# A graph attention layer on one core: GpSimd multiplies chunks 2 and 3 of x for the second table, in place of VectorE

## The reference

```python
in_fts = W @ x.T
f1 = (w1 @ in_fts).T + b1          # one number for each row
f2 = (w2 @ in_fts).T + b2          # one number for each column
bias_mat = where(adj > 0, 0.0, -1e9)
coefs = softmax(leaky_relu(f1 + f2.T) + bias_mat, axis=-1)   # slope 0.01
out = layernorm(x + coefs @ x, axis=-1)
```

## Time and profile before

| | |
|---|---|
| median of 3 runs | 275.73 us (275.19 to 277.98) |
| the profiled execution | 275.53 us, its span 273.8 us |
| busy share: PE, PEld, DVE, ACT, POOL | 94%, 82%, 89%, 72%, 23% |
| granted TensorE clock | full (mean 0.999) |
| HBM read, written | 71.37 MB, 2.10 MB |

### The profile page before, as it was taken

One profiled execution on the slowest core, in us unless ns is written; L12 is line 12 of the kernel. 1 busy time (PEld: TensorE's weight loads), 2 busy tenths in 40 slices (PEclk: granted clock), 3 DMA queues, 4 the chain that ended last, 5 costly groups with the idle time before them and its releaser, 6 DMA issues.

```text
span 273.8 us, 5925 instructions
## 1 busy us (share of the span) xinstructions
PE 257.2 (94%) x2163; PEld 223.8 (82%) x2163; DVE 244.6 (89%) x316; ACT 195.9 (72%) x285; POOL 64.0 (23%) x92
## 2 busy tenths in 40 slices
PE   2999969799999999999999999999999999999991
PEld 2989747688888888888888888888888888888880
DVE  1898999996998899999999999999999999999943
ACT  2669999939999999997499729982998196012140
POOL 2000045940000015201620063006300630063330
PEclk9999999999999999999999999999999999999999
DMA  6999999999999999999999999999999999501020
GB/s 188 275 294 314 321 323 284 263 260 314 329 326 327 328 327 326 346 345 328 316 331 342 327 302 230 339 315 314 293 347 326 320 238 341 143 0 38 1 60 19
DMA packets 22502, 73.64 MB, mean 269 GB/s; under 512 B 3030, under 2 KB 4184, under 8 KB 22488
## 3 DMA queue, kind: packets, MB, share of 16 engines
q1 hardware_dynamic: 11184, 35.17, 42.6%
q10 hardware_dynamic: 9960, 34.64, 41.4%
q0 software_dynamic: 1344, 3.67, 4.9%
HBM read 71.37 MB, written 2.10 MB: 268 GB/s over the span
## 4 chain that ended last, share of the span: by engine, by line
DVE 63%; DMA 12%; issue 10%; POOL 5%; ACT 5%; ACTq 1%; DVEq 1%; PE 0%; POOLq 0%
DVE mn L718 20%; DVE msk L731 11%; DVE mn L723 11%; DMA nat<-in_adj 11%; ACT sgn L462 4%; DVE post L839 3%; DVE ybt L854 2%; DVE bns L859 2%; DVE ntot L844 2%; DVE post L841 2%; DVE bt L708 2%; DVE post L702 2%; DMA msk<-in_x 1%; POOL ea L372 1%; DVE msk L736 1%
## 5 line engine op out<-in xcount | busy, mean ns | idle before, releaser
L1075 PE MATMUL ps<-bt,msk 128*128 128x258 f16 x2048 | 232.1, 274 | 4.5 <-DVE msk L731 2.8
L1075 PEld LDWEIGHTS ps<-bt,msk 128*128 128x128 fp8e5 x2048 | 200.6, 98 | 35.3 <-issue 4.1
L462 ACT ACTIVATE sgn<-f2b,nf1l 128x1024 int8<-128x1024 f32 x128 | 136.5, 1147 | 6.2 <-POOL flag L395 4.8
L718 DVE TENSOR_SCALAR mn<-nat 128x4096 int8<-128x4096 int32 x32 | 73.1, 2283 | 3.0 <-DMA nat<-in_adj 2.5
L402 POOL TENSOR_SCALAR nmr<-mv 128x4 f32<-128x4 f32 x7 | 12.8, 1834 | 141.1 <-DVE mv L863 141.1
L731 DVE STREAM_TRANSPOSE msk<-mn 128x1024 uint32<-128x1024 uint32 x32 | 39.8, 1245 | 2.6
L723 DVE SCALAR_TENSOR_TENSOR mn<-sgn,mn 128x1024 uint32<-128x1024 uint32 x32 | 39.2, 1225 | 3.3 <-ACT sgn L462 2.3
L591 ACT ACTIVATE ybt<-ybt,nmr,rstd 128x128 f32<-128x128 f32 x28 | 11.5, 483 | 33.2 <-POOL nmr L407 33.2
L584 ACT ACTIVATE post<-ps,ac 128x258 f32<-128x258 f32 x60 | 25.0, 471 | 14.1 <-PE ps L1075 14.1
L736 DVE TENSOR_SCALAR msk<-msk 128x1024 uint32<-128x1024 uint32 x32 | 22.2, 695 | 1.0
L413 POOL DMA_DIRECT2D out<-ybt x24 | 13.7, 570 | 16.3 <-ACT ybt L591 14.9
(11 more groups left out here) (109 smaller groups left out, 105.7 us busy)
## 6 DMA issues: line engine op xcount, KB each, us to landing
nat<-in_adj SPq DMA_DIRECT2D x64, 512.0 KB, 13.8
nat<-in_adj ACTq DMA_DIRECT2D x64, 512.0 KB, 16.3
xn<-in_x POOLq DMA_DIRECT2D x4, 512.0 KB, 19.8
out<-ybt POOLq DMA_DIRECT2D x24, 64.0 KB, 6.7
msk<-in_x SPq DMA_DIRECT2D x8, 128.0 KB, 3.8
msk<-in_x ACTq DMA_DIRECT2D x8, 128.0 KB, 4.5
out<-ybt SPq DMA_DIRECT2D x4, 64.0 KB, 1.8
out<-post SPq DMA_DIRECT2D x4, 32.0 KB, 1.6
```

What stands on the lines that cost most here:

```text
L462: ins = act.activation(sgn[:, c, g * JA:(g + 1) * JA], f2b[:, :], ACT.Sign, bias=nf1l[:, bass.ds(G * t + g, 1)], scale=-1.0)
L718: dve.tensor_scalar(mn[:, c % 2], nat[:, c], 0, EDGE, ALU.is_gt, ALU.mult).then_inc(cast_done, 1)
L1075: ins = pe.matmul(ps[:, 2 * c + m, 0:2 * DV], mask_f[c][m][:, n // KB, n % KB, :], btv[m][:, n, :], start=(n == 0), stop=(n == NK - 1))
```

## The change

The multiplies of chunks 2 and 3 for table m=0 leave VectorE's list and go to GpSimd's, as `tensor_tensor` with the same operands (128 x 1024 f32, both inputs in SBUF), ahead of its four loads of `xn` and of the flag's 17 instructions. Each waits for table_ready[1] to reach h+1, so for `low_x(1, 2)` and `low_x(1, 3)`. `split_x(0, 2)` and `split_x(0, 3)` wait for the new semaphore y_pool. `plus(0, 0)` moves one place forward on VectorE, to where `scale_x(0, 2)` stood. ScalarE's, TensorE's and SP's lists have the same instructions in the same order.

```diff
@@ GpSimd's list @@
+            pool.wait_ge(cs_ready[0], 1)
+            for h in range(2, BCH):
+                pool.wait_ge(table_ready[1], h + 1)
+                part = slice(h * CN, (h + 1) * CN)
+                pool.tensor_tensor(ybuf[:, h], xl_chunk(h), cs[:, 0, part, None].to_broadcast([P, CN, D]),
+                                   ALU.mult).then_inc(y_pool, 1)
+
             pool.wait_ge(f1_made, 2)
             pool.wait_ge(cast_done, 2)
             for g in range(G):
@@ split_x on ScalarE @@
                 elif m == 0:
-                    act.wait_ge(y_ready[0], h - 1)
+                    act.wait_ge(y_pool, h - 1)
@@ VectorE's list @@
             dve.wait_ge(cs_ready[0], 1)
             low_den(0)
-            scale_x(0, 2)
+            plus(0, 0)
             stat_max(1, 2, 4)
-            scale_x(0, 3)
-            plus(0, 0)
             low_x(0, 0)
@@
-            dve.wait_ge(y_ready[0], 2)
+            dve.wait_ge(y_pool, 2)
             turn(3, 3)
```

More of the change, by code:

```diff
@@ L200, in gat_kernel @@
         y_act = sem("y_act")
-        y_ready = [sem(f"y_ready{m}") for m in range(2)]
+        y_pool = sem("y_pool")
+        y_ready = sem("y_ready")
         hi_ready = [sem(f"hi_ready{m}") for m in range(2)]
@@ L510, in split_x @@
                 elif m == 0:
-                    act.wait_ge(y_ready[0], h - 1)
+                    act.wait_ge(y_pool, h - 1)
                 else:
-                    act.wait_ge(y_ready[1], h + 1)
+                    act.wait_ge(y_ready, h + 1)
                 act.activation(btv[m][:, h * CN:(h + 1) * CN, 0:D], ybuf[:, h], ACT.Copy,
@@ L698, in stat_out, with scale_x @@
                 dve.wait_ge(gst_ready, j + 1)
-            def scale_x(m, h):
+            def scale_x(h):
                 part = slice(h * CN, (h + 1) * CN)
-                dve.tensor_tensor(ybuf[:, h], xl_chunk(h), cs[:, m, part, None].to_broadcast([P, CN, D]),
-                                  ALU.mult).then_inc(y_ready[m], 1)
+                dve.tensor_tensor(ybuf[:, h], xl_chunk(h), cs[:, 1, part, None].to_broadcast([P, CN, D]),
+                                  ALU.mult).then_inc(y_ready, 1)
             def low_x(m, h):
@@ L773, in _ @@
             dve.wait_ge(cs_ready[1], 1)
-            scale_x(1, 0)
+            scale_x(0)
             stat_max(0, 0, 2)
-            scale_x(1, 1)
+            scale_x(1)
             stat_out(0, 0, 2)
@@ L783, in _ @@
             turn(0, 0)
-            scale_x(1, 2)
+            scale_x(2)
             low_x(1, 1)
-            scale_x(1, 3)
+            scale_x(3)
             low_x(1, 2)
```

## The result

The changed kernel takes **276.94 us** (median of 22 runs, 275.76 to 279.63), the kernel before in the same session 275.74 (22 runs, 274.35 to 277.98). The ratio is 1.0047, with a 95% interval of 1.0027 to 1.0067: half a per cent slower, clear of the noise, and inside the 1% that the prediction counts as no change. The profiled execution took 277.28 us with a span of 275.57.

The account below looks back on a forecast made before the run. The prediction took TensorE to bound the kernel: tile 2's start (52.75) + 215 + a tail of some 6 us. With no gain from relief and +0.5 at tile 2's start, 275.53 became 276.0 us; range 274.9 to 278.0.

Parts of the forecast that it names:

- What bounds it: From tile 2 on, TensorE's 1920 matmuls at 0.112 us each set the end; VectorE is second.
- What sets tile 2: Tile 2's start at 52.75 follows VectorE's transpose, behind ScalarE's unbroken work; VectorE has 0.30 us to spare.
- Part 1: Two multiplies removed from VectorE in the head, 2.28 us together; worth 0 at the end.
- Rival C: VectorE's relief reaches the end through earlier statistics, flag and tile 4 mask: up to 2.3 us faster, 273.2; chance 0.04.
- Part 2: Two multiplies added to GpSimd in the head, 2.1 us each; bounds 1.25 and 8.0 us.
- Part 3: The port in the head: GpSimd's multiplies hold VectorE too, shifting it 0.68 us and tile 2's start +0.5 us.
- rival A: The multiplies in the head fit in for nothing, by no hold or T near 1.25: 275.5 us; chance 0.22.
- Part 4: GpSimd's queue behind the multiplies: flag at 59.2, tile 4 in time with 0.6 us of cover, no cost.
- Nothing there waits: The xn loads, issued some 6 us later on GpSimd's queue, are needed only near 99 us: no cost.
- some 6 us: The tail added after tile 2's start and TensorE's 215 us of matmuls to give the end.
- The number: The forecast for the whole kernel: 275.53 + 0.5 = 276.0 us; chance 0.57.
- Rival B: GpSimd's queue becomes the bound: TensorE loses e - 41.7 us at tile 4, e ending the second multiply; chance 0.15.

Follow-up runs that it names:

- e3: The changed kernel with 20 spare TensorE matmuls into an unread bank, filling its wait for low_x(1,3): 276.08 us, 1.0022 of the kernel before.
- e4: The changed kernel with GpSimd's first multiply also waiting for combine(1,1), so it starts behind the cast: 276.15 us, 1.0021 of the kernel before.
- e11: The changed kernel run again without any edit, 12 runs: 276.82 us, 1.0020 of the kernel before.
- e1: The changed kernel with the two GpSimd multiplies left out, so only VectorE's relief remains: 275.27 us, 0.9983 of the kernel before.
- e5: The changed kernel with 20 spare matmuls and the four xn loads between GpSimd's multiplies, still waiting for the cast: 277.37 us, 1.0060 of the kernel before.
- e6: The changed kernel with the four xn loads issued behind the instruction that sets the flag: 281.96 us, 1.0207 of the kernel before.
- e8: The kernel before with only its xn loads held until scale_x(0,2) is done: 276.13 us, 1.0009 of the kernel before.
- e10: The changed kernel with the xn loads between GpSimd's multiplies, not waiting for the cast, no spare matmuls: 276.31 us, 1.0000 of the kernel before.
- e12: The kernel before with its xn loads not waiting for the cast, plus 14 spare TensorE matmuls: 276.09 us, 0.9998 of the kernel before.
- e9: The changed kernel with 20 spare matmuls and the xn loads between GpSimd's multiplies, not waiting for the cast: 276.14 us, 1.0009 of the kernel before.

## Why the prediction came out as it did

- **What bounds it: right.** TensorE's 0.1119 us a matmul held in every trace, and the end was tile 2's start plus 215 us plus the tail wherever TensorE had no later gap. It also explains the miss: the two terms of the cost are the first and the last of that sum.
- **What sets tile 2: right, and more exactly than claimed.** In seven traces, among them e3, e4 and one execution of the changed kernel (e11), tile 2 stands 12.41 to 12.43 us behind ScalarE's mark, although VectorE and GpSimd do different work in them.
- **Part 1, the relief is worth 0: right** (e1: 0.9983, tile 2 at 52.78). Rival C is out.
- **Part 2, 2.1 us a multiply: close.** 1.90, and 1.88 back to back in e4. The Trainium skill's 4497 ns for 2048 elements (GPSIMD Engine Reference, section 3.1; an estimate of 2.25) is further off; the measurement decides.
- **Part 3, the hold in both directions: right.** The cast takes 1.71 us more, `low_den` 0.41 more; in e4 `low_den` and `plus` 2.45. That removes rival A's first reason, no hold. Its outcome, tile 2 where it was, is what e3, e4 and e11 show. It bears out the half of the Trainium skill's rule (SBUF — State Buffer, "Who interferes with whom") that the trace before could not show: GpSimd, which started first, kept VectorE's cast waiting. The second multiply ended at 40.39, forecast 41.65. **The step that failed is what the shift does next.** I had holds of 2.1 and 0.86 us less 2.28 of relief, a shift of 0.68, and let it reach tile 2 through the transpose (0.68 - 0.30 + 0.1 = 0.5). Measured, the holds are 1.71 and 0.41, so the shift is -0.16, and where the clock stays up (e3) the transpose is not late. I gave TensorE's longer wait at 37.56 no price at all, since TensorE has idle time before tile 2. In the executions where its clock then stays down until 45, it uses up that idle time and 1.0 to 1.3 us more. The sum had +0.5 there, so that the forecast came near was luck.
- **Part 4, the flag and tile 4: right.** Flag 59.48 against 59.2 (in e11, where TensorE's statistics are not late, 58.08), tile 4 with 0.7 us to spare against 0.6; e5 shows what comes when it is used up. **"Nothing there waits" for the `xn` loads failed**, and with it the constant tail of "some 6 us": in the profile it is 6.88 for 6.08 and VectorE's slack 0.29 for 2.78. e6 proves that the place of these loads can cost (2.1%). For the smaller move of this change nothing shows it: e8 has the waits in its trace and no cost in its median, e10 and e12 have them with early loads, and the changed kernel's own second trace (e11) has a tail of 6.08. So the cause of the 0.80 is open; what the traces show is its way, by a late VectorE and SyncE's stores.
- **The number**: 276.0 against 276.94, +0.5 against a measured +1.2 us (0.7 to 1.8 by the interval). Both terms that were missing point up.
- **Two slips of arithmetic.** The prediction's 214.97 is 215.00 by its two rows, which changes nothing. Rival B's far end, e = 53.5, should by its own formula cost 53.5 - 41.7 = 11.8 us and so give 287.3, not 284.2.

What stays open: how the half per cent is split. In the traces it is 0.94 and 0.80. In the medians, taking away the clock's fall (e3) leaves 1.0022, taking away both (e9) 1.0009, but e10, which takes away neither in its trace, has 1.0000, so runs of this kind do not resolve the parts. The waits for `in_adj` also scatter among executions (3.0 and 4.9 us for the changed kernel itself), and the second set of runs of the changed kernel (e11) is by its own interval not apart from the kernel before. Nothing here shows why the clock comes back sooner in some executions.

## What to carry to other kernels

Before moving work off an engine, ask whether it has the slot that sets the end; here 2.28 us off VectorE were worth nothing, and GpSimd's multiplies took 2.1 to 2.5 us back from VectorE by holding it. When a feeder of TensorE is delayed, price what TensorE's longer pause does to its granted clock, even where it has idle time to give: the matmuls behind the pause can take nearly twice as long. Before reading a shift of a few tenths from two traces, take it from a mark that moves with the head: here the mark itself lay anywhere between 39.47 and 40.81. And count a bulk load's place in a queue for the other loads that it will run beside, not only for its reader, when it moves by much.

## What the runs showed of the hardware

- A GpSimd two-input multiply of 128x1024 f32 took 1.90 us alone. Started 0.05 us ahead of VectorE's int32-to-int8 cast of 128x4096, it stretched that from 2.28 to 3.99 us; it stretched `plus` (128x1024, uint32) from 0.69 to 2.43.
- The granted clock fell to 1.2 GHz in every trace in which TensorE had waited 1.89 us or more for `low_x(1,3)` (six, waits of 1.89 to 3.17), and in none in which that wait was 1.29 or less (eight). What lies between was not run. The Trainium skill (TensorE: Matmul & The Clock Gate, "HAM oscillation — how this bites in real kernels") describes a kernel whose bursts of matmuls, each behind a wait for data, start at the lower clock. These traces agree in part. In the changed kernel the 8 matmuls behind the wait of 1.89 us still took 1.07 us, as before; the clock fell as they ended (0.93 in 36:39), and the 16 at 40.09 took 3.60 for 1.95; in e11, behind a wait of 2.79, the 8 took 1.90.
- The same kernel showed the lower clock through 45 us in one execution and only to 42 in another, with 1.9 us between the two times.
- The issue of four loads of 512 KB on GpSimd's queue took 3.38 to 5.25 us in the runs here.
